# Cross-attention of a Perceiver block: value products in seven blocks of 9 and 10 tiles a head instead of eleven of 6, weighed 12 tiles later, and each head turned by transposes

## The chip, the cores and the metric

One core of one Trainium2 chip runs the whole program. The metric is device time in microseconds (us) of one launch, median of three runs; the profile is one further execution of the same program. The engines are TensorE (PE, with its weight loads as PEld), VectorE (DVE), ScalarE (ACT), GpSimd (POOL) and SyncE (SP, which only issues DMAs here).

## The reference, cut to what matters

Two Perceiver layers work on 512 tokens of width 512 with a context of 8192 tokens. Each layer is a cross-attention, a sequence mixer (a selective scan in the first, a delta rule in the second) and a mixture of experts. Only the two cross-attentions are touched:

```
q = layernorm(x) W_Q + b_Q ; k = ctx W_K + b_K ; v = ctx W_V + b_V      # 16 heads of 32
p = exp(q k^T / sqrt(32) - rowmax) ; head = (p v) / sum(p)               # 512 x 8192 per head
x = x + concat(heads) W_O + b_O
```

## The kernel before

Everything is in float32 accuracy. Queries and keys are split into a high and a low part and stacked, so that a score product has 96 or 97 rows of contraction. The engines run programs of their own, in the order in which the code issues them, and meet by semaphores; the order is written out by hand.

A head has KT = 64 tiles of 128 keys. For each tile, in the steady part of an attention:

- **first score** (`first_on_pe`, L775): queries by 512 keys, of the *next* head, 12 tiles ahead of where it must be finished; it goes into one of four PSUM banks. DVE takes its row maxima (L780), which is what frees the bank: PE's first score k waits for DVE's reading k-4.
- **second score** (`second_on_pe`, L797): 128 keys by 512 queries of this head, with the row maximum already subtracted by a 97th row of contraction (`qs`, filled by `send_row`). It goes into one of three banks; ACT takes the exponential into `pt` (L920), a ring of slots of 128x512. Second score n waits for exponential n-3.
- **weighing** (`weigh`): products of `pt` with the values, three tiles side by side on 32 columns of TensorE each (L810), and on the last 32 columns a product of ones with sums of `pt` (L814), which gives the sum of the exponentials. Three value products and one product of ones make a round; one round is two passes. All accumulate in one bank (`OUT_BANK`). To need one product of ones per round and not three, POOL first adds up the tiles of a block (`add_up`, L932 and L935) into `exp_sums`, which has two buffers.
- **end of a head**: ACT copies `OUT_BANK` to `partial` (`take_partial`, L902). PE multiplies it by a constant `fold` matrix (`finish_head`, L820), which adds the three column groups and turns the head at once: four products of 128x33 in two passes. DVE takes the reciprocal of the sum (L943), multiplies (L946) and adds the value bias (L950). PE may weigh block 0 of the next head only after L946 (`finished`).

Before, a block is 6 tiles (two rounds; two adds of 1024 elements on POOL), 11 blocks a head, the last of 4 tiles (one add). A block is weighed two blocks later (LAG = 2): PE does the 6 tiles of block b, first and second score in turn, and then weighs block b-2. The ring has 18 slots. `upto` tells up to which first score PE and DVE have come after each block.

In the last head there are no first scores left. There DVE does the adds of the odd blocks (`on_vector`), and PE does the first output products between the tiles (`output_early`, L858) after turning the rows of finished heads (`turn_heads`, L854, four 128x128 transposes; ACT copies them in `copy_turned`, L898). In head 0 ACT also writes four rows of ones into the keys of the other buffer (`ones_on_act`, L724), at tiles 12, 24, 36 and 48.

Of the kernel before, what the change touches and what calls it, by code (L numbers as in the profile page):

```python
# [9 lines left out]
ALU = mybir.AluOpType  # L10
# [497 lines left out]
class CrossAttention:  # L508
# [17 lines left out]
    RING = (LAG + 1) * BLOCK  # L526
    EARLY = UNITS + AHEAD
    ONES = (2, 4, 6, 8)
# [3 lines left out]
    EARLY_PRODUCTS = [(), (), (), (), (0,), (1,), (2,), (3,), (4,), (5, 6), (7, 8)]  # L532
    LATE_FIRST, LATE_NEXT, LATE_SCORES, NEXT_KEYS = 2, 2, 68, (8, 10)

    def __init__(self, c, A, S, x, l, late=None):
        self.c, self.A, self.S, self.x, self.l, self.late = c, A, S, x, l, late
        self.slots, self.upto = self.first_slots()
        self.begun, self.keys_stored = 0, []

    def adds(self, b):  # L540

        return -(-len(self.BLOCKS[b]) // self.ROUNDS) - 1

# [4 lines left out]
    def sums_to(self, h, b):  # L548

        mine = self.on_vector(h, b)  # L550
        n = sum(self.adds(j) for i in range(h + 1) for j in range(len(self.BLOCKS)) if (i, j) <= (h, b) and self.on_vector(i, j) == mine)
        return (self.sum_dve if mine else self.sum_pool).at(n)

    def slot(self, h, b):
        return (h * len(self.BLOCKS) + b) % (self.LAG + 1) * self.BLOCK

# [62 lines left out]
    def run(self):  # L619
        c, l = self.c, self.l  # L620
        with ExitStack() as st:
# [6 lines left out]
            self.bv = c.sb(st, f"bv{l}", [P, D])  # L628
# [8 lines left out]
            self.folded, self.inverse, self.finished, self.biased = c.signals(st, "head_folded total_inverse head_finished head_biased")  # L637
# [88 lines left out]
    def loads(self, sp):  # L726
# [8 lines left out]
        sp.dma_start(self.bv[:], self.A["bv"][self.l].partition_broadcast(P)).then_inc(*self.wo_in.up())  # L735
# [17 lines left out]

    def first_slots(self):


        units = [(h, i) for h in range(HEADS) for i in range(self.UNITS)]
        last = len(self.BLOCKS) - 1
        upto = {(h, b): min(len(units), self.UNITS + h * KT + tiles[-1] + 1 + self.AHEAD)
                - (self.BLOCK * (last - b) // last if h == 0 else 0)  # L760
                for h in range(HEADS) for b, tiles in enumerate(self.BLOCKS)}
        return units, upto
# [24 lines left out]
    def on_pe(self, pe):  # L787
# [11 lines left out]
        def weigh(h, b):  # L799
            tiles, slot, sums = self.BLOCKS[b], self.slot(h, b), (h * NB + b) % 2  # L800
            if b == 0:
                pe.wait_ge(*self.v_in[h % 2].at(h // 2 + 1))
            if b == 0 and h:
                pe.wait_ge(*self.finished.at(h))
            pe.wait_ge(*self.exp.at(h * KT + tiles[-1] + 1))
            if self.adds(b):
                pe.wait_ge(*self.sums_to(h, b))
            for r in range(self.ROUNDS):
                for g, i in enumerate(range(3 * r, min(3 * r + 3, len(tiles)))):
                    last = pe.matmul(bank[self.OUT_BANK][g * DH:(g + 1) * DH, :], vs[h % 2][:, tiles[i], :], pt[:, slot + i, :],  # L810
                                     start=b == 0 and r == 0, stop=tiles[i] + 3 >= KT)
                if r < len(tiles):
                    item = self.sums[:, sums, r, :] if self.adds(b) else pt[:, slot + r, :]
                    last = pe.matmul(bank[self.OUT_BANK][3 * DH:4 * DH, :], c.ones[:, 0:DH], item, start=b == 0 and r == 0, stop=b == NB - 1 and r == min(self.ROUNDS, len(tiles)) - 1)  # L814
            last.then_inc(*self.weighed.up())

        def finish_head(h):
            pe.wait_ge(*self.taken.at(h + 1))
            for t in range(TT):
                last = pe.matmul(bank[self.OUT_BANK][:, t * (DH + 1):(t + 1) * (DH + 1)], self.partial[:, t * P:(t + 1) * P], c.fold[:], start=True, stop=True)  # L820
            last.then_inc(*self.folded.up())

        def head(h):
            begun = self.upto[h - 1, NB - 1] if h else self.EARLY
# [6 lines left out]
            for b, tiles in enumerate(self.BLOCKS):  # L831
                todo = list(range(begun, self.upto[h, b]))
                begun = self.upto[h, b]
                for i, t in enumerate(tiles):
                    if todo:
                        self.first_on_pe(pe, todo.pop(0))
                    second_on_pe(h, t)
                    if i == 3 and h + 1 == HEADS:
                        output_early(b)
                    if i == 3 and b == self.LAG and h:  # L840
                        finish_head(h - 1)
                for k in todo:
                    self.first_on_pe(pe, k)
                if b >= self.LAG:
                    weigh(h, b - self.LAG)
                elif h:
                    weigh(h - 1, NB - self.LAG + b)

        def turn_heads(k):

            pe.wait_ge(*self.biased.at((k + 1) * HEADS // KD))
# [8 lines left out]
        def output_early(b):  # L860

            if b == 0:
                pe.wait_ge(*self.first_read.at(HEADS * self.UNITS))
            if b < self.EARLY_OUT:
                turn_heads(b)
            for i in self.EARLY_PRODUCTS[b]:
# [15 lines left out]
        for b in range(NB - self.LAG, NB):  # L882
            weigh(HEADS - 1, b)
# [8 lines left out]
    def on_act(self, act):  # L892
        NB = len(self.BLOCKS)

        def copy_turned(k):
            b = k if k < self.EARLY_OUT else self.SECOND_BANK + 1
            act.wait_ge(*self.at_turned.at(k + 1))
            act.copy(self.at[:, k, :], self.c.bank[b]).then_inc(*self.at_copied.up())  # L898
# [10 lines left out]
        for h in range(HEADS):  # L909
            for b, tiles in enumerate(self.BLOCKS):  # L910
                if b == self.LAG and h:
                    take_partial(h - 1)
                if h + 1 == HEADS and 2 <= b < 2 + self.EARLY_OUT:
                    copy_turned(b - 2)
                if h == 0 and b in self.ONES:
                    self.ones_on_act(act, 1, self.ONES.index(b))
                for i, t in enumerate(tiles):
                    n = h * KT + t
                    act.wait_ge(*self.second.at(n + 1))
                    act.activation(self.pt[:, self.slot(h, b) + i, :], self.c.bank[self.SECOND_BANK + n % self.SECOND_ROOM], ACT.Exp).then_inc(*self.exp.up())  # L920
# [3 lines left out]
    def add_up(self, engine, h, b, n, signal):  # L924

        tiles, g, slot, R = self.BLOCKS[b], h * len(self.BLOCKS) + b, self.slot(h, b), self.ROUNDS
        engine.wait_ge(*self.exp.at(h * KT + tiles[min((n + 2) * R, len(tiles)) - 1] + 1))
        to = self.sums[:, g % 2]
        if n == 0:
            if g > 1:  # L930
                engine.wait_ge(*self.weighed.at(g - 1))
            engine.tensor_tensor(to, self.pt[:, slot:slot + R, :], self.pt[:, slot + R:slot + 2 * R, :], ALU.add).then_inc(*signal.up())  # L932
        else:
            engine.wait_ge(*signal.at(signal.total - signal.base))
            engine.tensor_tensor(to, to, self.pt[:, slot + (n + 1) * R:slot + (n + 2) * R, :], ALU.add).then_inc(*signal.up())  # L935

    def on_dve(self, dve):
        bank = self.c.bank

        def finish_head(h):  # L940
            folded = bank[self.OUT_BANK][:, 0:TT * (DH + 1)].rearrange("p (t d) -> p t d", t=TT)
# [1410 lines left out]
```

## Time and profile before

| what | value |
|---|---|
| median of 3 runs | 3646.66 us (3643.27 to 3648.98) |
| the profiled execution, its own time | 3645.09 us |
| its span, first to last instruction | 3643.3 us (1.8 us lie around it) |
| mean granted TensorE clock | 0.984 |
| PE / DVE / ACT / POOL busy, share of the span | 97% / 69% / 54% / 49% |
| first attention, from its first second score to its last weighing | 700 to 1561 us |
| second attention | 1995 to 2855 us |

Busy shares over the whole span mix stages. The two attentions are some 1720 us of the 3643 us; the stages before, between and after them are the same in both kernels. A time such as 1101.51 is the start of an instruction in us from the start of the span; the second column of the order of time is how long it, or the run of equal instructions, took. A matmul's row is longer than its share of the engine, since matmuls overlap: what one costs is the distance between the starts of two.

### The profile page before, as it was taken

The numbers are of one execution on the slowest core, as the hardware profiler recorded it, in microseconds if no ns is written. First come the engines' busy times: TensorE is split into PE (matmuls) and PEld (weight loads), VectorE is DVE, ScalarE is ACT, GpSimd is POOL, SyncE is SP. The second block draws the span as 40 slices with busy tenths as digits, with TensorE's granted clock in tenths as the row PEclk, the third lists the DMA queues.
The fourth block names the chain that finished last, engine by engine and source line by source line (L and its number), as shares of the span: only waits on it lengthen the run. The fifth ranks groups of instructions, "written<-read, shape, count | busy, mean of one in ns | idle before, by whom it ended". The sixth has DMA issues, their size and how long they took to land. (4 is left out here: it accounts for less than half of the span.)

```text
span 3643.3 us, 47301 instructions
## 1 busy us (share of the span) xinstructions
PE 3527.5 (97%) x17916; PEld 2334.9 (64%) x17916; DVE 2497.3 (69%) x3465; ACT 1967.2 (54%) x3024; POOL 1773.3 (49%) x744
## 2 busy tenths in 40 slices
PE   8999999999999999988999999999999897999999
PEld 6788787755555555446876555555554476788887
DVE  3222344478777777457996777777775565899998
ACT  2122322366666666634972666666666322777786
POOL 2222222399999999700000999999998320100001
PEclk9999999999999999998998999999999998999999
DMA  7777776633333333046977433333330101999998
GB/s 272 253 243 235 234 239 208 190 79 91 93 90 77 88 93 77 15 174 223 359 302 238 122 92 84 80 93 93 80 91 24 53 1 53 361 377 374 374 375 302
DMA packets 249729, 628.50 MB, mean 173 GB/s; under 512 B 43633, under 2 KB 137873, under 8 KB 194977
## 3 DMA queue, kind: packets, MB, share of 16 engines
q1 hardware_dynamic: 210720, 552.08, 46.8%
q10 hardware_dynamic: 36864, 67.13, 5.0%
q0 software_dynamic: 1920, 6.29, 0.5%
q8 instruction: 143, 2.34, 0.3%
q14 instruction: 82, 0.66, 0.1%
HBM read 488.46 MB, written 136.87 MB: 172 GB/s over the span
## 5 line engine op out<-in xcount | busy, mean ns | idle before, releaser
L780 DVE TENSOR_REDUCE maxima<-psum 128x1 f32<-128x512 f32 x2048 | 1263.4, 680 | 359.3 <-PE psum L775 359.1
L920 ACT ACTIVATE pt<-psum 128x512 f32<-128x512 f32 x2048 | 1047.7, 612 | 590.6 <-PE psum L797 587.9
L932 POOL TENSOR_TENSOR exp_sums<-pt 128x1024 f32<-128x1024 f32 x342 | 819.3, 2396 | 259.2 <-ACT pt L920 136.9
L775 PE MATMUL psum<-ks,first_q 96*128 96x512 f32 x2048 | 852.4, 416 | 0.8
L797 PE MATMUL psum<-qs,ks 97*128 97x512 f32 x2048 | 817.7, 406 | 12.2 <-ACT pt L920 9.1
L935 POOL TENSOR_TENSOR exp_sums<-exp_sums,pt 128x1024 f32<-128x1024 f32 x310 | 735.7, 2373 | 44.5
L810 PE MATMUL psum<-pt,vs 128*32 128x512 f32 x4096 | 673.9, 598 | 2.1 <-POOL exp_sums L932 1.9
L814 PE MATMUL psum<-exp_sums,constants 128*32 128x512 f32 x1408 | 669.8, 598 | 0.0
L775 PEld LDWEIGHTS psum<-ks,first_q 96*128 96x128 f32 x2048 | 390.0, 190 | 354.2 <-DVE maxima L780 236.2
L1631 DVE TENSOR_TENSOR moe_cut<-moe_raw,moe_cut 128x2048 fp32r<-128x2048 f32 x244 | 556.8, 2289 | 55.9 <-ACT moe_cut L1627 49.5
L1627 ACT CAST moe_cut<-moe_raw 128x2048 fp32r<-128x2048 f32 x244 | 469.0, 1923 | 56.2 <-PE psum L97 47.3
L797 PEld LDWEIGHTS psum<-qs,ks 97*128 97x128 f32 x2048 | 390.7, 192 | 128.4 <-ACT pt L920 48.8
L372 POOL TENSOR_TENSOR cparts<-cx,cparts 128x2048 fp32r<-128x2048 f32 x32 | 147.7, 4615 | 522.3 <-ACT cparts L285 522.3
L810 PEld LDWEIGHTS psum<-pt,vs 128*32 128x32 f32 x4096 | 139.4, 109 | 342.3 <-issue 231.2
L1539 POOL DMA_INDIRECT ln_m_rows<-y_slots,row_of x8 | 14.0, 1747 | 666.4 <-DMA y_slots<-moe_yrow 664.6
L354 DVE SCALAR_TENSOR_TENSOR kparts<-psum,bk,kparts 128x512 fp32r<-128x512 f32 x128 | 96.0, 750 | 276.1 <-ACT kparts L311 276.1
L95 PE MATMUL psum<-moe_cut,moe_xg 128*128 128x512 f32 x608 | 241.6, 397 | 3.8 <-DVE moe_xg L1699 3.8
L97 PE MATMUL psum<-moe_cut,moe_xg 128*128 128x512 f32 x608 | 237.4, 390 | 0.0
L96 PE MATMUL psum<-moe_cut,moe_xg 128*128 128x512 f32 x608 | 236.6, 389 | 0.0
L95 PE MATMUL psum<-cparts,wk_high 128*128 128x512 f32 x512 | 205.7, 402 | 19.9 <-POOL cparts L372 16.9
L311 ACT ACTIVATE kparts<-psum,bk 128x512 fp32r<-128x512 f32 x128 | 88.0, 688 | 245.3 <-PE psum L97 221.9
L285 ACT CAST cparts<-cx 128x2048 fp32r<-128x2048 f32 x32 | 61.0, 1908 | 265.0 <-PE psum L97 178.4
(334 smaller groups left out, 4526.5 us busy)
## 6 DMA issues: line engine op xcount, KB each, us to landing
moe_raw<-in_moe_w SPq DMA_DIRECT2D x244, 1024.0 KB, 7.9
ks<-k_parts SPq DMA_DIRECT2D x384, 256.0 KB, 4.6
k_parts<-kparts ACTq DMA_DIRECT2D x256, 256.0 KB, 4.4
cx<-in_ctx SPq DMA_DIRECT2D x32, 1024.0 KB, 6.1
vs<-v_heads SPq DMA_DIRECT2D x32, 1024.0 KB, 5.3
v_heads<-vrow SPq DMA_DIRECT2D x25, 1024.0 KB, 5.1
late_context<-cparts SPq DMA_DIRECT2D x28, 512.0 KB, 11.6
late_parts<-late_context SPq DMA_DIRECT2D x28, 512.0 KB, 4.7
```

The source lines that it names most:

```text
L95: pe.matmul(out, lhs[0], rhs[0], start=start, stop=False)
L97: return pe.matmul(out, lhs[1], rhs[0], start=False, stop=stop)
L775: pe.matmul(self.c.bank[self.FIRST_BANK + k % self.FIRST_ROOM], self.first_q[s][:, t * P:(t + 1) * P], self.ks[s][part][0:3 * DH, at:at + ...
L780: dve.tensor_reduce(self.maxima[:, h % 2, i % TT, i // TT:i // TT + 1], self.c.bank[self.FIRST_BANK + k % self.FIRST_ROOM], X, ALU.max).th ...
L797: pe.matmul(bank[self.SECOND_BANK + n % self.SECOND_ROOM], ks[h % 2][part][:, at:at + P], qs[h % 2][:], start=True, stop=True).then_inc(*s ...
L810: last = pe.matmul(bank[self.OUT_BANK][g * DH:(g + 1) * DH, :], vs[h % 2][:, tiles[i], :], pt[:, slot + i, :], start=b == 0 and r == 0, st ...
L814: last = pe.matmul(bank[self.OUT_BANK][3 * DH:4 * DH, :], c.ones[:, 0:DH], item, start=b == 0 and r == 0, stop=b == NB - 1 and r == min(se ...
L920: act.activation(self.pt[:, self.slot(h, b) + i, :], self.c.bank[self.SECOND_BANK + n % self.SECOND_ROOM], ACT.Exp).then_inc(*self.exp.up())
L932: engine.tensor_tensor(to, self.pt[:, slot:slot + R, :], self.pt[:, slot + R:slot + 2 * R, :], ALU.add).then_inc(*signal.up())
L935: engine.tensor_tensor(to, to, self.pt[:, slot + (n + 1) * R:slot + (n + 2) * R, :], ALU.add).then_inc(*signal.up())
L1627: act.copy(self.cut[:, g % self.CUT, 0], self.raw[:, g % self.RAW]).then_inc(*self.high.up())
L1631: dve.tensor_tensor(self.cut[:, g % self.CUT, 1], self.raw[:, g % self.RAW], self.cut[:, g % self.CUT, 0].bitcast(F32), ALU.subtract).then ...
```

## The change

A block has nine tiles (three rounds) and the seventh and last has ten (four rounds, the last of one tile). POOL adds three tiles at once: two adds of 1536 elements a block, 14 a head. The product of ones of the tenth tile's round takes `pt` itself. A block is no longer weighed at a block's end but after the second score of the tile 12 behind its last tile, which is after tiles 20, 29, 38, 47 and 56 of the head and 1 and 11 of the next. The ring has 24 slots and the heads lie 66 slots apart, so that three tiles that are added together never wrap around. First scores are given out tile by tile (`first_to`), not block by block. In the diff below, the first `finish_head` is PE's and the second DVE's, which is now issued after the first score of tile 17 (`TURN + 1`); the lines with `later` are of `add_up`, whose n is 0 and 1.

The end of a head is done without `fold`: PE turns `partial` by four 128x128 transposes (after tile 16), DVE multiplies all three groups by the reciprocal into `scaled` and adds the groups by a reduction. Weighing the next head's block 0 waits for the multiplication (`divided`). The value bias is added later, as the bias of `copy_turned`. The row bias `x + b_O` in heads 0 to 3 stays. `SHARED` is empty, so no add is shared between POOL and DVE.

```diff
-    ROUNDS, LAG = 2, 2
+    ROUNDS, LAG = 3, 12
     BLOCK = 3 * ROUNDS
-    BLOCKS = [list(range(t, min(t + 3 * 2, KT))) for t in range(0, KT, 3 * 2)]
+    BLOCKS = [list(range(t, t + 3 * 3)) for t in range(0, KT - 10, 3 * 3)] + [list(range(KT - 10, KT))]
+    STRIDE, RING = 66, 24
+    TAKE, TURN = LAG, LAG + 4
+    SHARED, SHARE_AT = (), 3
-    RING = (LAG + 1) * BLOCK
-    ONES = (2, 4, 6, 8)
+    ONES = (12, 24, 36, 48)
+    COPY_AT = (10, 15, 20)
+    EARLY_AT = {3: (0, ()), 8: (1, ()), 13: (2, ()), 26: (None, (0,)), 32: (None, (1,)), 38: (None, (2,)), 43: (None, (3,)), 48: (None, (4,)), 53: (None, (5, 6)), 58: (None, (7, 8))}
...
+    def slot(self, h, t):
+        return (h * self.STRIDE + t) % self.RING
+    def due(self, h, t, late):
+        n = h * KT + t - late
+        return [(n // KT, b) for b, tiles in enumerate(self.BLOCKS) if n >= 0 and n % KT == tiles[-1]]
+    def first_to(self, h, t):
+        n = self.UNITS + h * KT + t + 1 + self.AHEAD - (6 * (KT - 1 - t) // (KT - 7) if h == 0 else 0)
+        return min(len(self.slots), max(self.EARLY, n))
...
         def finish_head(h):
             pe.wait_ge(*self.taken.at(h + 1))
             for t in range(TT):
-                last = pe.matmul(bank[self.OUT_BANK][:, t * (DH + 1):(t + 1) * (DH + 1)], self.partial[:, t * P:(t + 1) * P], c.fold[:], start=True, stop=True)
+                last = pe.transpose(bank[self.OUT_BANK][:, t * P:(t + 1) * P], self.partial[:, t * P:(t + 1) * P], c.ident[:])
...
+            for t in range(KT):
+                for k in range(begun, self.first_to(h, t)):
+                    self.first_on_pe(pe, k)
+                begun = self.first_to(h, t)
+                second_on_pe(h, t)
+                if h + 1 == HEADS and t in self.EARLY_AT:
+                    output_early(*self.EARLY_AT[t])
+                if t == self.TURN and h:
+                    finish_head(h - 1)
+                for block in self.due(h, t, self.LAG):
+                    weigh(*block)
...
-            act.copy(self.at[:, k, :], self.c.bank[b]).then_inc(*self.at_copied.up())
+            act.activation(self.at[:, k, :], self.c.bank[b], ACT.Identity, bias=self.bv[:, k:k + 1]).then_inc(*self.at_copied.up())
...
+        later = self.slot(h, tiles[3 * n + 3])
+        engine.wait_ge(*self.exp.at(h * KT + tiles[3 * n + 3] + hi))
+            engine.tensor_tensor(to, self.pt[:, first + lo:first + hi, :], self.pt[:, later + lo:later + hi, :], ALU.add).then_inc(*signal.up())
...
         def finish_head(h):
-            dve.tensor_tensor(rows, folded[:, :, 0:DH], self.total[:, :, None].to_broadcast([P, TT, DH]), ALU.mult).then_inc(*self.finished.up())
+            dve.tensor_tensor(self.scaled[:].rearrange("p t g d -> p t (g d)"), turned[:, :, 0:3 * DH], self.total[:, :, None].to_broadcast([P, TT, 3 * DH]), ALU.mult).then_inc(*self.divided.up())
+            dve.tensor_reduce(self.rows[:, :, h * DH:(h + 1) * DH], self.scaled[:].rearrange("p t g d -> p t d g"), X, ALU.add).then_inc(*self.finished.up())
-            dve.tensor_tensor(rows, rows, self.bv[:, None, h * DH:(h + 1) * DH].to_broadcast([P, TT, DH]), ALU.add).then_inc(*self.biased.up())
```

## Rows read from the trace of the kernel before

**Rows 1.** The page, busy time: engine, us, share of the span, instructions.

```profile
PE 3527.5 (97%) x17916; PEld 2334.9 (64%) x17916; DVE 2497.3 (69%) x3465; ACT 1967.2 (54%) x3024; POOL 1773.3 (49%) x744
```

**Rows 2.** Busy time by stretch: heads 1 to 14 of the first attention.

```profile
760.00:1490.00 730.00, 730.00 (x4205) 394.53 (x4205) 571.32 (x933) 454.47 (x888) 679.56 (x287) 1.00 0.33 84
```

**Rows 3.** Order of time on PE, one steady block.

```profile
1101.51 0.50 PE L775 MATMUL psum<-ks,first_q 96*128 96x512 f32 x1
1101.84 0.39 PE L797 MATMUL psum<-qs,ks 97*128 97x512 f32 x1
...
1104.18 0.40 PE L797 MATMUL psum<-qs,ks 97*128 97x512 f32 x1
...
1105.39 0.60 PE L810 MATMUL psum<-pt,vs 128*32 128x512 f32 x3
...
1105.82 0.60 PE L810 MATMUL psum<-pt,vs 128*32 128x512 f32 x3
...
1106.37 0.50 PE L775 MATMUL psum<-ks,first_q 96*128 96x512 f32 x1
```

**Rows 4.** Order of time, DVE and ACT beside that block.

```profile
1102.04 3.68 DVE L780 TENSOR_REDUCE maxima<-psum 128x1 f32<-128x512 f32 x6 [1.18 <-PE psum L775]
...
1102.27 3.05 ACT L920 ACTIVATE pt<-psum 128x512 f32<-128x512 f32 x6 [1.81 <-PE psum L797]
```

**Rows 5.** Order of time on DVE: a head's first block, an end of head, six heads on.

```profile
1130.23 3.68 DVE L780 TENSOR_REDUCE maxima<-psum 128x1 f32<-128x512 f32 x6 [1.43 <-PE psum L775]
...
1142.62 0.29 DVE L946 TENSOR_TENSOR head_rows<-psum,total 128x128 f32<-128x128 f32 x1
1142.94 1.79 DVE L950 TENSOR_TENSOR head_rows<-head_rows,bv 128x128 f32<-128x128 f32 x1
...
1450.60 3.68 DVE L780 TENSOR_REDUCE maxima<-psum 128x1 f32<-128x512 f32 x6 [1.43 <-PE psum L775]
```

**Rows 6.** Order of time on PE: fold in head 8, transposes in head 15.

```profile
1141.39 0.97 PE L820 MATMUL psum<-constants,partial 128*128 128x33 f32 x8
1142.20 0.48 PE L775 MATMUL psum<-ks,first_q 96*128 96x512 f32 x1
...
1503.96 0.60 PE L854 MATMUL psum<-constants,head_rows 128*128 128x128 f32 x4
1504.31 0.79 PE L797 MATMUL psum<-qs,ks 97*128 97x512 f32 x2
```

**Rows 7.** Costliest groups, whole trace: busy and mean ns, idle before.

```profile
L372 POOL TENSOR_TENSOR cparts<-cx,cparts 128x2048 fp32r<-128x2048 f32 x32 | 147.7, 4615 | 522.3 <-ACT cparts L285 522.3
L785 DVE TENSOR_REDUCE neg_max<-maxima 128x4 fp32r<-128x64 f32 x32 | 7.1, 220 | 1.1
L974 DVE TENSOR_TENSOR x_rows<-psum,x_rows 128x512 f32<-128x512 f32 x8 | 5.4, 678 | 8.3 <-PE psum L858 8.3
```

**Rows 8.** Order of time on POOL, first adds of two blocks without a wait.

```profile
1480.38 2.40 POOL L932 TENSOR_TENSOR exp_sums<-pt 128x1024 f32<-128x1024 f32 x1
...
1485.25 2.42 POOL L932 TENSOR_TENSOR exp_sums<-pt 128x1024 f32<-128x1024 f32 x1
```

**Rows 9.** Order of time in head 0 of the second attention, tile 12.

```profile
2003.36 1.89 ACT L724 CAST ks<-constants 1x2048 fp32r<-1x2048 f32 x1
...
2005.93 0.50 PE L797 MATMUL psum<-qs,ks 97*128 97x512 f32 x1 [1.35 <-ACT pt L920]
```

**Rows 10.** Order of time, last head of the first attention: ACT's step, then its end.

```profile
1495.06 3.05 ACT L920 ACTIVATE pt<-psum 128x512 f32<-128x512 f32 x6 [1.40 <-PE psum L797]
1499.50 2.07 ACT L920 ACTIVATE pt<-psum 128x512 f32<-128x512 f32 x4 [1.40 <-PE psum L797]
...
1551.95 2.07 ACT L920 ACTIVATE pt<-psum 128x512 f32<-128x512 f32 x4 [1.43 <-PE psum L797]
1556.85 2.36 POOL L932 TENSOR_TENSOR exp_sums<-pt 128x1024 f32<-128x1024 f32 x1 [5.95 <-PE psum L814]
1561.32 0.59 ACT L902 COPY partial<-psum 128x512 f32<-128x512 f32 x1 [7.30 <-PE psum L814]
```

More of the change, by code:

```diff
@@ L799, in weigh @@
         def weigh(h, b):
[L800 removed]
+            tiles, sums = self.BLOCKS[b], (h * NB + b) % 2
             if b == 0:
@@ L803, in weigh @@
             if b == 0 and h:
-                pe.wait_ge(*self.finished.at(h))
+                pe.wait_ge(*self.divided.at(h))
             pe.wait_ge(*self.exp.at(h * KT + tiles[-1] + 1))
[L806 to L814, printed above, removed]
+            if not self.on_vector(h, b):
+                pe.wait_ge(*self.sum_pool.at(self.sums_by_pool(h, b)))
+            if self.on_vector(h, b) or self.shared(h, b):
+                pe.wait_ge(*self.sum_dve.at(self.sums_by_dve(h, b)))
+            rounds = [tiles[i:i + 3] for i in range(0, len(tiles), 3)]
+            for r, three in enumerate(rounds):
+                for g, t in enumerate(three):
+                    pe.matmul(bank[self.OUT_BANK][g * DH:(g + 1) * DH, :], vs[h % 2][:, t, :], pt[:, self.slot(h, t), :], start=b == 0 and r == 0, stop=t + 3 >= KT)
+                item = self.sums[:, sums, r, :] if r < self.ROUNDS else pt[:, self.slot(h, three[0]), :]
+                last = pe.matmul(bank[self.OUT_BANK][3 * DH:4 * DH, :], c.ones[:, 0:DH], item, start=b == 0 and r == 0, stop=b == NB - 1 and r == len(rounds) - 1)
             last.then_inc(*self.weighed.up())
@@ L881, in on_pe @@
             head(h)
-        for b in range(NB - self.LAG, NB):
-            weigh(HEADS - 1, b)
+        for t in range(KT, KT + self.LAG):
+            for block in self.due(HEADS - 1, t, self.LAG):
+                weigh(*block)
         finish_head(HEADS - 1)
@@ L909, in on_act, with add_up @@
         for h in range(HEADS):
-            for b, tiles in enumerate(self.BLOCKS):
-                if b == self.LAG and h:
+            for t in range(KT):
+                n = h * KT + t
+                if t == self.TAKE and h:
                     take_partial(h - 1)
[L913 to L920, printed above, removed]
+                if h + 1 == HEADS and t in self.COPY_AT:
+                    copy_turned(self.COPY_AT.index(t))
+                if h == 0 and t in self.ONES:
+                    self.ones_on_act(act, 1, self.ONES.index(t))
+                act.wait_ge(*self.second.at(n + 1))
+                act.activation(self.pt[:, self.slot(h, t), :], self.c.bank[self.SECOND_BANK + n % self.SECOND_ROOM], ACT.Exp).then_inc(*self.exp.up())
         take_partial(HEADS - 1)
         copy_turned(KD - 1)
[L924 to L928, printed above, removed]
+    def add_up(self, engine, h, b, n, signal, parts=range(3)):
+        g, tiles, lo, hi = h * len(self.BLOCKS) + b, self.BLOCKS[b], parts[0], parts[-1] + 1
+        later = self.slot(h, tiles[3 * n + 3])
+        to = self.sums[:, g % 2, lo:hi]
+        engine.wait_ge(*self.exp.at(h * KT + tiles[3 * n + 3] + hi))
         if n == 0:
@@ L931, in add_up @@
                 engine.wait_ge(*self.weighed.at(g - 1))
[L932 to L935 removed]
+            first = self.slot(h, tiles[0])
+            engine.tensor_tensor(to, self.pt[:, first + lo:first + hi, :], self.pt[:, later + lo:later + hi, :], ALU.add).then_inc(*signal.up())
+        else:
+            engine.tensor_tensor(to, to, self.pt[:, later + lo:later + hi, :], ALU.add).then_inc(*signal.up())
     def on_dve(self, dve):
@@ L2239, in perceiver @@
         const = c.sb(ctx, "constants", [P, CONST_COLS])
-        c.ident, c.ones, c.iota, c.upto, c.lower, c.level0, c.fold, c.spare = (
-            const[:, CONST_AT[n][0]:CONST_AT[n][1]] for n in ("ident", "ones", "iota", "upto", "lower", "level0", "fold", "spare"))
+        c.ident, c.ones, c.iota, c.upto, c.lower, c.level0, c.spare = (
+            const[:, CONST_AT[n][0]:CONST_AT[n][1]] for n in ("ident", "ones", "iota", "upto", "lower", "level0", "spare"))
         c.level_t = [const[:, CONST_AT["level_t"][0] + k * P:CONST_AT["level_t"][0] + (k + 1) * P] for k in range(LEVELS)]
```

113 lines of the change are left out of this document (47 added, 66 removed).

## The prediction

> **What bounds the kernel now.** I read the page's busy times first: PE is busy for 97% of the span, and no other engine comes near [rows 1]. That share says nothing of a stage, so I went to the busy time by stretch. In heads 1 to 14 PE is busy for all of the 730 us at the full clock (1.00, the 2.4 GHz level), POOL for 679.56 (93%), DVE for 78%, ACT for 62%, the DMA engines for 33% [rows 2]. So PE sets the attention's pace, with POOL close behind it. The chain of waits adds nothing there, since PE waits for nobody. What a block costs PE is read from the order of time [rows 3]: the block repeats after 1106.37 - 1101.51 = 4.86 us. Eleven starts of scores in turn lie (1104.18 - 1101.84)/10 = 0.234 us apart, and one pass of weighing takes 1105.82 - 1105.39 = 0.43. Twelve scores (2.81) and four passes (1.72) make 4.53, so 0.33 us of each block is neither: it is the change from scores to weighing and back (the first score after weighing stands 0.33 ahead of the second and not 0.234, the rest lies at the two edges). Six heads take 1450.60 - 1130.23 = 320.37 us, 53.4 a head [rows 5]. The sum for one: 128 scores 30.0, 44 passes 18.9, 11 changes 3.6, end of head 0.8, together 53.3. The steady part is understood.
>
> **The change, part by part.**
>
> *Blocks.* 64 tiles in threes are 22 rounds before and after, so the number of products stays. The changes between scores and weighing go from 11 to 7 a head. Up to tile 51 of head 14, where first scores end, a layer weighs 14x11+7 = 161 times before and 14x7+4 = 102 after: 59 x 0.33 = 19.5 us, for two layers **-39.1 us** (0.331 unrounded). All of it lies on PE's path.
>
> *Longer runs between two weighings.* Runs of 6 become runs of 9, one of 10. PE steps by 0.469 a tile, DVE by (3.68-0.68)/5 = 0.60 and ACT by (3.05-0.61)/5 = 0.488 [rows 4], so both fall behind in a run and recover in the weighing. DVE starts 0.53 after the first score; first score k (from 0) wants to start at 0.10+0.469k and needs reading k-4, which ends at 0.53+0.60(k-4)+0.68. They meet at k = 9.8, at 9.4 with 0.06 us for the semaphore; the longest run has k = 9. For ACT, with three banks, they meet beyond k = 20. Cost taken: 0; if the slack of DVE fails, below.
>
> *POOL.* Without a wait two adds of 1024 take 1485.25 - 1480.38 = 4.87 us [rows 8]. An add of 2048 elements took 4.615 us elsewhere [rows 7], against 2.40, so 512 more elements cost 1.11. A pair of 1536 then takes 4.87+2.2 = 7.1, at most 1.5x4.87 = 7.3. PE needs 18x0.234+6x0.43+0.33 = 7.12 for nine tiles and 8.45 for the block of ten. Seven pairs are 49.7 (51.1) us a head against PE's 51.8 (53.4 less 4x0.33 and 0.46, plus 0.2, as below): POOL stays behind PE. A pair can begin with the sixth exponential of its block and is wanted about 9.1 us later (two runs and the weighing between them, less what leads up to it), so a drift of 0.18 a block is absorbed. Cost 0. The Trainium skill (Perfetto Trace Analysis, GPSIMD Engine Instruction) says that spans of GpSimd are unreliable and that start-to-start spacing is to be used; by the spans a pair before would be 4.8, by spacing it is 4.87, which is what I take, and neither makes POOL the bound.
>
> *End of a head on PE.* The fold keeps the next score off for 1142.20 - 1141.39 = 0.81 us, four transposes of the same size for 1504.31 - 1503.96 = 0.35 [rows 6]. 28 heads end in the steady part: 28x0.46 = **-12.9 us**; at 0.60 for the transposes it would be -6.
>
> *The wait on DVE.* PE may weigh block 0 only after the multiplication. It now has 384 elements: between 128 (0.29, [rows 5]) and 512 (0.678, [rows 7]) that is 0.55. In the run of tiles 12 to 20, DVE has read tile 17's scores 0.53+3.68 = 4.21 after the run's start, the reciprocal takes 0.2, the multiplication 0.55, a semaphore about 0.06: 5.03. PE comes to the weighing at 0.33+8x0.469+0.35+0.09+0.33 = 4.86. So a new stall of 0.2 us a head, 28x0.2 = **+5.6 us** (0 to 0.5 a head: 0 to 14). Behind that wait stand the rest of PE's queue; ACT and DVE have idle time there. The reduction that follows reads 384 elements of SBUF; one of 64 took 0.22 on the mean of 32 beside a busy POOL [rows 7], one of 512 some 0.68 (the short runs of [rows 4] end so), so some 0.55, where the bias add that goes had 1.79 [rows 5]. DVE has 1.5 us a run to spare, so neither counts.
>
> *The row bias add of heads 0 to 3* has two inputs in SBUF, as the bias add that goes away. That one, small as it is, took 1.79 because it waited for POOL's running add [rows 5]. The row bias add will now meet adds of 3.5 us. In its place POOL's first add of block 1 ends some 0.4 us after DVE gets there, and DVE is back before PE needs it: 0; if it waits for the second add too, 2.5 us eight times, 20 us. The Trainium skill (SBUF — State Buffer, "Who interferes with whom") says that a DVE instruction with two SBUF inputs contends with a GpSimd one that reads SBUF, and that a reduction does not on this chip; the trace agrees on both. If that were wrong for the reduction, see the third rival.
>
> *Ones in head 0.* Before, the copies at tiles 24, 36 and 48 stand behind a weighing, where ACT is idle. Now tile 24 is fourth in a run. A copy of 1.89 in the middle of a run held PE for 1.35 [rows 9] (tile 12, in both kernels). Tile 36 is seventh, and its late exponentials are wanted only after the weighing. Two layers: **+3 us**. Head 0 also has its first weighing after 21 tiles, not 18; three more tiles at DVE's step instead of PE's: 3x0.13x2 = **+1 us**.
>
> *The last head.* Here ACT is the slower one: a block of six steps by 1499.50 - 1495.06 = 4.44 us, with 1.40 idle during weighing [rows 10]. Nine tiles with three rounds: 4.44+3x0.488+0.86 = 6.76, against 6.66; over 76 tiles +0.8. The three copies of turned heads now stand in the middle of runs, each 0.5 on ACT's path, before mostly in its idle time: +1.2. At the end, before, the last exponential is done at 1554.02, and the copy of the head starts at 1561.32, 7.3 later. After, POOL's first add can start four tiles before the last exponential is done (-1.95), two adds take 7.15, and from its end to the copy it was 1561.32 - 1559.21 = 2.11 for four passes, so 3.83 for eight: 9.0, +1.7. The transposes and the longer DVE end give back 0.5. Together 3.2 a layer, **+6.5 us** (2 to 12).
>
> The bias on the copy of turned heads costs nothing visible: it is one ACT instruction for another. The smaller load of the bias is off the path.
>
> **Sum.** -39.1-12.9+5.6+3+1+6.5 = -35.9 us. On the profiled execution's own 3645.09 that gives 3609; that execution lies 1.6 below the median of 3646.66, so the forecast is 3611.
>
> **The rivals.**
> 1. *DVE's four banks don't carry the longer runs.* For: DVE's step is 28% longer than PE's, and the slack at k = 9 is only 0.05 to 0.1 us by the sum above. Against: at k = 5 the slack before is 0.6, and no wait shows. If nothing beyond six tiles were covered, 22 tiles a head would cost 0.13 each, 2.9 us a head, 30 heads 88 us, and the kernel would be slower (3699). It decides from 1.6 us a head on. The likelier form is a part of it, 0.1 to 0.2 a run, or a longer wait for the multiplication: 3623 to 3640.
> 2. *POOL becomes the pace*, the other side. If three tiles at once cost more per element (a pair over 7.4 us), PE waits in `weigh` for POOL; over 7.63 (53.4/7) the head is longer than before. At 7.8: 54.6 a head, +1.2x30, 3683. For: POOL is 93% busy. Against: the add of 2048 at 2.25 ns an element, below 2.34 for 1024.
> 3. *The reduction waits for POOL as the old bias add did.* In the gap between POOL's adds it costs nothing; waiting out the second add it is some 2.3 us a head, 28 heads 64 us: 3675.
> 4. *More than the sum*: no stall at the multiplication, last head at its lower end: -46, 3600 or just below.
>
> **How the numbers follow.** Forecast (3600 to 3622) 0.71; a partial stall of the first rival 0.13, its full form 0.03; POOL 0.04; the reduction 0.03; better 0.06. The likeliest is 3611. From 3600 I reach up to 3632, which takes in the upper bounds of the unknown costs (8 more at the wait, 7 at the transposes, 6 in the last head) and the nearer half of the partial stall. A change within 0.2% (7.3 us) is about what this measurement can't tell from none: faster than 3639.4 for 0.88, between for 0.04, slower for 0.08.
>
> **What the profile after would show.** A steady head of 51.8 us; nine tiles every 7.12 us on PE; no idle time of PE before first and second scores, and 0.2 us of it before block 0 is weighed; POOL adds of 3.5 us with small waits for ACT, not PE waiting for POOL; 102 weighings before the last stretch. The prediction is wrong if a switch does not cost 0.33 in the longer block (then nine tiles take over 7.2), if PE shows waits for DVE in runs, or if POOL's pair is over 7.4.

## The result and the profile after

The changed kernel takes 3618.73 us (median of 4 runs, 3611.42 to 3621.58), the kernel before beside it 3644.97: ratio 0.9925 (95% interval 0.9912 to 0.9937), which is 26 us less by the medians and 27 by the ratio. Forecast were 3611 and 36 less, in a range of 3600 to 3632. Two more series of the same kernel gave 0.9925 and 0.9924. The profiled execution took 3621.58 us, its span is 3619.6, 23.7 below the span before.

The page after, busy times, and the stretch that answers to [rows 2]:

```profile
PE 3495.2 (97%) x17788; PEld 2344.2 (65%) x17788; DVE 2462.6 (68%) x3457; ACT 1956.6 (54%) x3024; POOL 1751.4 (48%) x528
```

```profile
760.00:1442.00 682.00, 681.16 (x3989) 381.99 (x3991) 533.85 (x898) 431.03 (x855) 641.49 (x185) 1.00 0.35 88
```

PE is busy throughout as before, at the full clock; POOL has 94%. The page's 528 and 744 count all of POOL's instructions; the adds of exponentials among them are now 436 (2 x 218, shown below) and were 652. Next, the order of time on PE, one steady run of nine tiles with its weighing, beside [rows 3]:

```profile
1101.49 0.50 PE L785 MATMUL psum<-ks,first_q 96*128 96x512 f32 x1
1101.82 0.40 PE L807 MATMUL psum<-qs,ks 97*128 97x512 f32 x1
...
1105.58 0.39 PE L807 MATMUL psum<-qs,ks 97*128 97x512 f32 x1
1105.90 0.63 PE L823 MATMUL psum<-pt,vs 128*32 128x512 f32 x3
...
1108.61 0.50 PE L785 MATMUL psum<-ks,first_q 96*128 96x512 f32 x1
```

1108.61 - 1101.49 = 7.12 us for nine tiles, where the sum said 7.12: eighteen starts of scores 0.234 apart (4.21), six passes of 0.43 (2.58) and 0.33 for the change. The eight steps between second scores are (1105.58 - 1101.82)/8 = 0.470 each, so PE does not wait within the run. The next run is longer, 1115.91 - 1108.61 = 7.30. DVE in it, against [rows 4], shows why: the reduction for the row maximum (L795) falls among its readings, so the ninth first score waits for its bank. It starts 0.30 after the second score ahead of it and the second score after it another 0.34, where each was 0.23; together these are the 0.18, within the rounding:

```profile
1109.16 2.48 DVE L790 TENSOR_REDUCE maxima<-psum 128x1 f32<-128x512 f32 x4 [1.66 <-PE psum L785]
1111.67 0.22 DVE L795 TENSOR_REDUCE neg_max<-maxima 128x4 fp32r<-128x64 f32 x1
1111.81 3.07 DVE L790 TENSOR_REDUCE maxima<-psum 128x1 f32<-128x512 f32 x5
```

```profile
1112.24 0.40 PE L807 MATMUL psum<-qs,ks 97*128 97x512 f32 x1
1112.54 0.50 PE L785 MATMUL psum<-ks,first_q 96*128 96x512 f32 x1
1112.88 0.39 PE L807 MATMUL psum<-qs,ks 97*128 97x512 f32 x1
...
1115.91 0.49 PE L785 MATMUL psum<-ks,first_q 96*128 96x512 f32 x1
```

The end of a head on DVE, beside [rows 5], with reciprocal, multiplication of 384 elements and reduction (0.17, 0.56, 0.60, forecast 0.2, 0.55, 0.55):

```profile
1132.06 3.68 DVE L790 TENSOR_REDUCE maxima<-psum 128x1 f32<-128x512 f32 x6 [2.44 <-PE psum L785]
1135.66 0.17 DVE L951 RECIPROCAL total<-psum 128x4 f32<-128x4 f32 x1
1135.86 0.56 DVE L953 TENSOR_TENSOR scaled<-psum,total 128x384 f32<-128x384 f32 x1
1136.45 0.60 DVE L955 TENSOR_REDUCE head_rows<-scaled 128x128 f32<-128x384 f32 x1
```

And on PE, beside [rows 6]: the four transposes keep the next score off for 1134.32 - 1133.96 = 0.36 us, and the weighing of block 0 starts 0.46 after the last second score and not 0.33, so it waits 0.13 for the multiplication:

```profile
1133.96 0.60 PE L831 MATMUL psum<-constants,partial 128*128 128x128 f32 x4
1134.32 0.51 PE L785 MATMUL psum<-ks,first_q 96*128 96x512 f32 x1
...
1136.06 0.40 PE L807 MATMUL psum<-qs,ks 97*128 97x512 f32 x1
1136.52 0.63 PE L823 MATMUL psum<-pt,vs 128*32 128x512 f32 x3
```

POOL's groups on the page show 3.49 us for an add of 1536 elements (forecast 3.50), and that POOL waits for exponentials. PE waits for POOL 6.9 us in all, at the ends of the two attentions:

```profile
L941 POOL TENSOR_TENSOR exp_sums<-pt 128x1536 f32<-128x1536 f32 x218 | 760.8, 3490 | 275.2 <-ACT pt L927 270.1
L943 POOL TENSOR_TENSOR exp_sums<-exp_sums,pt 128x1536 f32<-128x1536 f32 x218 | 761.8, 3494 | 17.2
L823 PE MATMUL psum<-pt,vs 128*32 128x512 f32 x4096 | 652.7, 599 | 8.7 <-POOL exp_sums L943 6.9
```

The end of the first attention, in order of time, against [rows 10]:

```profile
1534.65 2.56 ACT L927 ACTIVATE pt<-psum 128x512 f32<-128x512 f32 x5 [1.10 <-PE psum L807]
...
1538.87 3.42 POOL L943 TENSOR_TENSOR exp_sums<-exp_sums,pt 128x1536 f32<-128x1536 f32 x1
...
1542.43 0.63 PE L823 MATMUL psum<-pt,vs 128*32 128x512 f32 x3 [3.44 <-POOL exp_sums L943]
...
1544.78 1.14 PE L823 MATMUL psum<-pt,vs 128*32 128x512 f32 x3
1545.63 1.14 PE L823 MATMUL psum<-pt,vs 128*32 128x512 f32 x3
...
1547.81 0.59 ACT L910 COPY partial<-psum 128x512 f32<-128x512 f32 x1 [10.60 <-PE psum L825]
```

From the last exponential (1537.21) to the copy of the head it is 10.6 us; before it was 7.3, forecast were 9.0. PE waits 3.44 us for POOL's two adds. After that wait its passes lie 0.43 us apart at first and then 0.85 (1545.63 - 1544.78): the granted clock has gone to its 1.2 GHz level. Busy time by stretch shows 0.68 for these 5.4 us:

```profile
1542.40:1547.80 5.40, 5.34 (x28) 1.58 (x28) 0.00 (x0) 0.00 (x0) 0.00 (x0) 0.68 0.01 3
```

Before the change PE waited there too, but only 0.97 us, and the passes after it lay 0.43 apart:

```profile
1559.35 0.63 PE L810 MATMUL psum<-pt,vs 128*32 128x512 f32 x3 [0.97 <-POOL exp_sums L932]
...
1559.78 0.63 PE L810 MATMUL psum<-pt,vs 128*32 128x512 f32 x3
```

ACT's copies of the heads to `partial` cut every trace into the same stretches. The table has them for all kernels, in us (the experiments are described below). Head 0 counts from the first second score; "steady head" is the mean of the 13 from the copy of head 0 to that of head 13, second attention.

| kernel | steady head | head 0, 2nd att. | head 0, 1st att. | heads 14, 15, 2nd att. |
|---|---|---|---|---|
| before | 53.48 | 63.20 | 64.60 | 51.57, 49.88 |
| after | 52.01 | 64.85 | 69.98 | 50.97, 53.20 |
| after_again | 52.02 | 64.84 | 67.00 | 51.01, 53.17 |
| after_third | 52.02 | 64.27 | 70.41 | 51.03, 53.19 |
| blocks_only | 52.34 | 64.97 | 68.81 | 52.97, 53.11 |
| transposes_only | 53.36 | 63.22 | 67.87 | 51.44, 49.90 |
| split_rounds | 54.51 | 66.58 | 68.61 | 51.77, 52.78 |
| turn_14 | 53.64 | 64.96 | 67.01 | 53.33, 53.19 |
| ones_behind | 52.04 | 62.29 | 65.32 | 52.73, 53.19 |
| last_on_dve | 52.02 | 64.90 | 67.04 | 50.98, 48.02 |
| ahead_16 | 51.85 | 65.41 | 69.29 | 52.42, 53.18 |
| three_edits | 51.85 | 62.50 | 66.87 | 52.34, 48.04 |

The steady heads gain 1.47 x 13 = 19.1 us in each attention. Head 0 gives back 1.65 in the second attention, head 15 3.3, head 14 gains 0.6: -14.7 in all. The first attention gains 11.0, since its head 0 is 5.4 longer. Outside the attentions the profiled execution is 2.0 longer.

One difference in the last column isn't the code's alone. In some attentions head 14 takes 52.3 to 53.3 us instead of 51.0 to 51.8, and then its mean clock is 0.97 and not 1.00. That is so in 9 of the 20 attentions of kernels with the new blocks (in one of the changed kernel's own six), and in none of the four of `before` and transposes_only. No wait of PE over 0.4 us stands in such a head (ones_behind, 1439 to 1496 us), so what brings the clock down there stays open.

### The profile page after: what moved, and what is told of

The parts are those of the page before. It is cut to its first block and busy times, and to the rows that moved or that the text cites. A ratio compares the mean times of both kernels' runs of the same rounds, so it can differ in the third digit from the quotient of the medians.

```text
span 3619.6 us, 46469 instructions
## 1 busy us (share of the span) xinstructions
PE 3495.2 (97%) x17788; PEld 2344.2 (65%) x17788; DVE 2462.6 (68%) x3457; ACT 1956.6 (54%) x3024; POOL 1751.4 (48%) x528
## 5 line engine op out<-in xcount | busy, mean ns | idle before, releaser
L927 ACT ACTIVATE pt<-psum 128x512 f32<-128x512 f32 x2048 | 1036.0, 625 | 520.6 <-PE psum L807 518.0
L941 POOL TENSOR_TENSOR exp_sums<-pt 128x1536 f32<-128x1536 f32 x218 | 760.8, 3490 | 275.2 <-ACT pt L927 270.1
L943 POOL TENSOR_TENSOR exp_sums<-exp_sums,pt 128x1536 f32<-128x1536 f32 x218 | 761.8, 3494 | 17.2
L823 PE MATMUL psum<-pt,vs 128*32 128x512 f32 x4096 | 652.7, 599 | 8.7 <-POOL exp_sums L943 6.9
L825 PE MATMUL psum<-exp_sums,constants 128*32 128x512 f32 x1344 | 622.6, 599 | 0.0
L823 PEld LDWEIGHTS psum<-pt,vs 128*32 128x32 f32 x4096 | 156.4, 110 | 377.1 <-issue 313.8
```

Source lines behind the costliest of these rows:

```text
L927: act.activation(self.pt[:, self.slot(h, t), :], self.c.bank[self.SECOND_BANK + n % self.SECOND_ROOM], ACT.Exp).then_inc(*self.exp.up())
L941: engine.tensor_tensor(to, self.pt[:, first + lo:first + hi, :], self.pt[:, later + lo:later + hi, :], ALU.add).then_inc(*signal.up())
L943: engine.tensor_tensor(to, to, self.pt[:, later + lo:later + hi, :], ALU.add).then_inc(*signal.up())
```

## The experiments

**after_again, after_third: the changed kernel once more.** No edit.

> The changed kernel once more, for the clock. In the profile after, the granted clock stood at the 1.2 GHz level for 20.5 us from the start of the first attention, before the change for 10.2 us, and again for 3.4 us where the end of each attention waits for POOL. Theory: the steady head takes 52.0 us again, and the 3.4 us at the end of each attention comes back, since the wait before it does; the length at the start is chance, so it may be 10 or 20 us, and the first head of the first attention then takes 66 or 70 us. Rival: the longer low stretch belongs to the change and is 20 us again in every profile of it, head 70 us, and it explains 4 us of the shortfall by itself. Time 3612 to 3621 either way.

> The changed kernel beside it, on the same chip: 0.9925 of the kernel before, steady head 52.0. Its low-clock stretch at the start of the first attention is 10 or 20 us by chance (one more profile for that count).

Measured: 3615.75 us (ratio 0.9925, 0.9912 to 0.9939) and 3619.09 (0.9924, 0.9911 to 0.9938). The steady head is the same to 0.01 us. Head 0 of the first attention took 67.00 and 70.41. Busy time by stretch of the first 40 us of that attention, the clock in the third column from the right; in this order after, after_again, after_third:

```profile
697.60:737.60 40.00, 37.64 (x154) 21.66 (x155) 24.59 (x39) 28.37 (x45) 27.25 (x8) 0.75 0.66 175
```

```profile
697.60:737.60 40.00, 36.69 (x166) 21.45 (x166) 27.09 (x44) 30.79 (x50) 29.66 (x9) 0.87 0.66 175
```

```profile
698.00:738.00 40.00, 37.52 (x152) 21.16 (x153) 24.05 (x38) 27.77 (x44) 26.78 (x8) 0.74 0.67 174
```

The same kernel has 0.74, 0.75 or 0.87 there, and its head 0 is 3 us longer at the lower ones. transposes_only had 0.76, with blocks as before. So the longer low stretch doesn't need the change, and the change doesn't always bring it. How often either kernel has it can't be said from one profile each of before and the variants. The mean clock of whole runs says a little more: 25 runs of the kernel before have 0.982 to 0.985 (mean 0.984), the 14 of the changed kernel 0.980 to 0.983 (mean 0.982). By my estimate the two low stretches at the ends of the attentions, 3.4 us each at half the clock, make 0.001 of that; the other 0.001, some 4 us, is not accounted for. So chance alone at the start is not shown either. The low stretch behind the wait for POOL was there at both ends in all three profiles; it begins between at once and some 1.3 us after the end of the wait, and costs about four passes of 0.43.

**blocks_only: the end of a head as before.**

```diff
-                last = pe.transpose(bank[self.OUT_BANK][:, t * P:(t + 1) * P], self.partial[:, t * P:(t + 1) * P], c.ident[:])
+                last = pe.matmul(bank[self.OUT_BANK][:, t * (DH + 1):(t + 1) * (DH + 1)], self.partial[:, t * P:(t + 1) * P], c.fold[:], start=True, stop=True)
...
+            dve.tensor_tensor(rows, rows, self.bv[:, None, h * DH:(h + 1) * DH].to_broadcast([P, TT, DH]), ALU.add).then_inc(*self.finished.up())
```

> The changed kernel with the end of a head as before: fold products on PE, multiplication of 128 elements and bias add on DVE. Theory: PE loses 0.46 us a head at the fold and gets back the 0.15 us that it now waits for the longer multiplication: 52.3 us a head against 52.0, 28 heads +9 us, so about 3628. Rival: the longer multiplication, the reduction and the transposes together cost what the fold did (DVE is late by them for the rest of the run), so the head stays at 52.0 and the time within 3 us of the changed kernel. A third way: the bias add waits for a POOL add of 3.5 us now, not 2.4, and DVE holds PE up: over 52.6 a head, over 3637.

Measured: 3628.00 us (ratio 0.9959, 0.9945 to 0.9973), steady head 52.34. The theory holds: the new end of a head is worth 0.32 us of each, the new blocks the rest, 53.48 - 52.34 = 1.14 (from head 5 on 53.39 - 52.33 = 1.06). Four changes fewer (1.32) less the 0.17 of the long run are 1.15 by the sum, so no gain is left over for the later weighing, the larger ring and the first scores tile by tile, which came with the blocks. The bias add took 1.14 us on DVE in head 8 (in order of time from 1140.20), less than the 1.79 before. In both kernels it ended about 0.15 us after the end of the POOL add that was running when it started (1141.19 here, 1144.58 before), so what it takes depends on where in POOL's add it starts.

**transposes_only: the other half alone, on the kernel before.** The same lines the other way round.

> The kernel before with the end of a head by transposes, multiplication of 384 elements and reduction, blocks of 6 as before. Theory: PE saves 0.46 us, but the head is turned after the fourth tile of a run and block 0 is weighed after the sixth, so PE comes to it at 0.33+5*0.469+0.44+0.33 = 3.45 us after the run's start and DVE is through at 3.01+0.2+0.55+0.06 = 3.82: it waits 0.37. Head 53.3 against 53.4, time 3640 to 3645. Rival: the transposes carry a good part of the change's gain by themselves (0.46 a head and no wait), 53.0 a head, 3633.

Measured: 3637.98 us (ratio 0.9989, 0.9980 to 0.9998), steady head 53.36, and from head 5 on 53.27 to 53.33, against 53.35 to 53.43 before. The saved 0.46 us of fold is nearly all lost to the wait for the multiplication, as the sum of the theory had it (0.37): in the order of time on PE block 0 is weighed 1142.89 - 1142.21 = 0.68 us after the last second score and not 0.33. Most of the change is the blocks.

**split_rounds: the changes between scores and weighing put back, nothing else.** `SPLIT` is (1, 2, 3, 4).

```diff
-                for block in self.due(h, t, self.LAG):
-                    weigh(*block)
+                for r in range(3):
+                    for i, b in self.due(h, t, self.LAG + 3 * r):
+                        if b in self.SPLIT:
+                            weigh(i, b, r)
+                        elif r == 0:
+                            weigh(i, b)
```

> The changed kernel with blocks 1 to 4 of each head weighed in three pieces, one round each, after the tiles 12, 15 and 18 behind the block's last one, and not three rounds at a stretch. Nothing is added but changes between scores and weighing: 8 more a head. Theory (a change costs 0.33 us): +2.65 us a head, less 0.16 for the shorter runs where DVE no longer is late: 54.5 a head, 30 heads +75 us, about 3694. Rival (the blocks' gain comes from elsewhere, from fewer and longer adds on POOL, and the change between scores and weighing hides): 52.0 a head, 3619. In between, a change costs less when a single round stands between scores.

Measured: 3684.72 us (ratio 1.0119, 1.0103 to 1.0134), steady head 54.51, where the theory said 54.5. The order of time on PE has a piece of three tiles with one round in 1109.40 - 1106.80 = 2.60 us: six scores 1.40, two passes 0.86, and 0.34:

```profile
1106.80 0.50 PE L786 MATMUL psum<-ks,first_q 96*128 96x512 f32 x1
...
1109.40 0.50 PE L786 MATMUL psum<-ks,first_q 96*128 96x512 f32 x1
```

POOL's adds are the same here as in the changed kernel, so their number is not what the change gains from; the price of a change is what it is. The total is 69 us over the changed kernel (3615.75) and not 75, since only 26 steady heads have all eight: 26 x 2.49 are 65, and head 0 and head 14 add 1.7 and 0.8 in the second attention.

**turn_14: DVE's end of head earlier in the run.**

```diff
-    TAKE, TURN = LAG, LAG + 4
+    TAKE, TURN = LAG, LAG + 2
```

> The changed kernel with the head turned after tile 14 and not 16, DVE's end of head after tile 15's scores. Theory of the four banks: PE no longer waits 0.15 us for the multiplication, but DVE's 1.3 us now stand after the fourth reading of the run; its fifth ends at 3.0+1.3+0.68 = 5.0 us after the run's start, and the ninth first score, which wants to start at 4.3, waits for it: +0.75-0.15, so 52.6 us a head against 52.0. Rival: only the wait for the multiplication counts, since DVE has idle time in each run: 51.9 us a head.

Measured in one run: 3665.38 us. From head 5 on a head takes 52.67 to 52.84, near the 52.6 of the four banks. Heads 1 to 4, where DVE also does the row bias add, take 54.78 to 56.53, which neither theory had. In the order of time on DVE that add (L959) takes 2.12 us in head 1, in the changed kernel 1.01, and the same within 0.03 in the other seven; the first fence is turn_14, with the POOL add that was running, the second the changed kernel:

```profile
766.28 3.46 POOL L941 TENSOR_TENSOR exp_sums<-pt 128x1536 f32<-128x1536 f32 x1 [0.99 <-ACT pt L927]
768.17 2.12 DVE L959 TENSOR_TENSOR x_rows<-x_rows,bo 128x512 f32<-128x512 f32 x1
```

```profile
772.88 1.01 DVE L959 TENSOR_TENSOR x_rows<-x_rows,bo 128x512 f32<-128x512 f32 x1
```

It ends at 770.29, behind the end of POOL's add at 769.74, and PE waits 2.62 us for DVE. In the next head the wait is the same, but what follows it is not:

```profile
770.95 0.63 PE L785 MATMUL psum<-ks,first_q 96*128 96x512 f32 x1 [2.62 <-DVE maxima L790]
...
772.79 1.07 PE L823 MATMUL psum<-pt,vs 128*32 128x512 f32 x3
773.65 1.07 PE L823 MATMUL psum<-pt,vs 128*32 128x512 f32 x3
...
827.33 0.50 PE L785 MATMUL psum<-ks,first_q 96*128 96x512 f32 x1 [2.63 <-DVE maxima L790]
...
828.44 0.61 PE L823 MATMUL psum<-pt,vs 128*32 128x512 f32 x3
828.87 0.61 PE L823 MATMUL psum<-pt,vs 128*32 128x512 f32 x3
```

Passes are 0.86 us apart after the first wait and 0.43 after the second. Busy time by stretch for the two heads has the clock at 0.97 and at 1.00:

```profile
763.90:820.30 56.40, 53.77 (x307) 29.14 (x305) 42.48 (x69) 32.90 (x65) 49.12 (x15) 0.97 0.33 82
820.30:875.20 54.90, 52.27 (x306) 29.02 (x306) 42.49 (x69) 32.95 (x66) 49.18 (x15) 1.00 0.33 85
```

PE's wait is 2.62 to 2.65 us in all eight such heads; five of them have 0.97 and take 56.3 to 56.5 us, three have 1.00 and take 54.8. So the add costs 2 us a head by itself, and another 1.6 where the clock falls. The prediction had priced a late row bias add at 2.5 us a head and taken it as 0: at tile 16 the phase is good, at tile 14 it isn't.

**ones_behind, last_on_dve, ahead_16: one loss each.** Each is a single run without a run of the changed kernel beside it, so the stretches of its trace are read and not its time. The edits in this order:

```diff
-    ONES = (12, 24, 36, 48)
+    ONES = (21, 30, 39, 48)
...
-        return h + 1 == HEADS and b % 2 == 1
+        return h + 1 == HEADS and b % 2 == 0
...
-    AHEAD = 12
+    AHEAD = 16
```

> The changed kernel with ACT's four copies of ones in head 0 at tiles 21, 30, 39 and 48, each first after a weighing, and not at 12, 24, 36 and 48. Theory: the copies at tiles 12 and 24 each hold PE for 1.35 to 1.5 us in the second attention's first head, which goes from 64.8 to 62.0 to 63.3 us (the lower if DVE then keeps up in the long first run), and all other heads stay. Rival: ACT and DVE are so far behind in the first run of 21 tiles that the copies hide behind DVE: 64.5 or more.

Measured: head 0 of the second attention 62.29 us against 64.84 (3618.35 us in one run). The two waits of PE in that head, which the changed kernel's order of time shows, are gone:

```profile
1994.65 0.50 PE L807 MATMUL psum<-qs,ks 97*128 97x512 f32 x1 [1.60 <-ACT pt L927]
...
2005.33 0.50 PE L807 MATMUL psum<-qs,ks 97*128 97x512 f32 x1 [1.36 <-ACT pt L927]
```

The first is of tile 12 and was there before the change [rows 9]; the second, of tile 24, is new. What was gained did not show in the one time taken: head 14 was 1.6 and 1.8 longer in the two attentions, for a low stretch of the clock there (0.97 on the mean of the head).

> The changed kernel with the last head's blocks 0, 2, 4 and 6 added up by DVE and 1, 3 and 5 by POOL, the other way round. Theory: the last weighing waits 3.4 us for POOL's two adds of 3.5 us, and the clock falls to its 1.2 GHz level in that wait, which doubles four passes (+1.7). With DVE's adds of 1.76 us the wait goes and with it the low stretch: last head 48.0 us against 53.2 in both attentions, -10 us in all. Rival: the clock falls there anyway, as PE's share of busy time is low in the whole last head: 49.7. Second rival: DVE's adds wait for POOL's, or another end is late next: 51 or more.

Measured: last head 48.02 us in both attentions, and 3607.62 us in one run. The wait for POOL and the low stretch behind it are both gone: in the order of time the last passes lie 0.43 us apart and the copy follows 0.67 us after the last pass starts:

```profile
1539.06 0.59 PE L823 MATMUL psum<-pt,vs 128*32 128x512 f32 x1
1539.49 0.59 PE L823 MATMUL psum<-pt,vs 128*32 128x512 f32 x1
```

So the clock fell for the wait, and not for PE's lower share of busy time in the whole last head. Three_edits, below, shows it again in both attentions.

> The changed kernel with first scores 16 tiles ahead and not 12, so that the reduction for the row maximum comes after the ninth reading of a run (tile 47), where DVE is idle next, and not after the fourth (tile 51). Theory: that run takes 7.12 us like the others and not 7.30: 51.85 us a head against 52.02. Rival: the 0.17 us are lost elsewhere in the head (at the longest run, or where POOL's adds begin), and the head stays at 52.0. Four first scores move from the first attention's last head to the stage before it, at no cost to the sum.

Measured: steady head 51.85 us, as said; the time of the one run, 3620.51, doesn't show it. Head 14 was 1.3 and 1.4 longer, again with the clock at 0.97 in it.

**three_edits: these three together.**

> The changed kernel with three of the edits together: ones at tiles 21, 30, 39 and 48, the last head's blocks 0, 2, 4 and 6 on DVE, first scores 16 tiles ahead. Theory: they sit in different stretches and add up. 13 heads of 51.86 and not 52.02 in each attention (-4), head 0 shorter by 1.7 and 2.6 (-4), last head 48.0 and not 53.2 (-10): 18 us below the changed kernel, ratio to the kernel before 0.9875, about 3597 beside a kernel before of 3642.6. Rival: what is gained at one place is lost again to the granted clock, whose low stretches differ from run to run: within 10 us of the changed kernel, 3606 or more.

Measured: 3602.49 us (ratio 0.9884, 0.9869 to 0.9899), 16.6 below the changed kernel's 3619.09 beside it, where 18 were expected (as a ratio 0.9875, as a time 3597). The single stretches came as said: steady head 51.85, head 0 62.50, last head 48.04. Head 14 has 52.36 and 52.34 and not 51.0, with the clock at 0.97; that takes back 2.7 us, which is the rival in part. This is the fastest version.

## Why the prediction came out as it did

- **What bounds the kernel**: PE, before and after. Right.
- **Blocks, 0.33 us for each change between scores and weighing**: right in mechanism and size. The run of nine took the 7.12 us of the sum, and eight changes put back cost 2.49 us a head, which is 8 x 0.33 less the 0.17 below. One miscount: the trace before has 160 weighings up to the last first score of a layer and not 161, so the term is -38.4 and not -39.1.
- **End of a head on PE**: 0.45 us forecast less, 0.36 against 0.81 measured. Right.
- **The wait for the multiplication**: 0.2 us forecast, 0.13 to 0.15 measured. Blocks_only gives the balance of this and the last point as 0.32 us a head, the forecast had 0.26.
- **Longer runs, cost 0**: this step was too low. I set DVE's readings against four banks and found 0.05 to 0.1 us of slack at the ninth score, but left out that in one run of each head the reduction for the row maximum stands among them. The term was taken as 0 and measured 0.17 us a head (ahead_16), some 5 us in all. The run of ten took 1131.52 - 1123.02 = 8.50, against 8.45. The first rival named this form of loss, with 0.1 to 0.2 us for every run; it is one run in seven. In that run PE does wait for DVE, which the prediction had named as a sign of being wrong; but 0.17 us a head is a tenth of the 1.6 from which it would have decided.
- **POOL**: 3.49 us an add, no wait of PE in the steady part. Right; the second rival fell. In split_rounds its adds are unchanged and the time is not.
- **The reduction beside POOL**: 0.60 us each time (591 to 608 ns over 32), so it doesn't wait; the third rival fell. The row bias add takes 1.0 and costs PE nothing at tile 16 (heads 1 to 4 take 51.9 to 52.1 us like the others). What I had not counted: heads 1 to 4 were 0.27 us longer than the others before (53.6 to 53.7 against 53.4) and no longer are, a gain of 2 us.
- **Head 0**: +2 us a layer forecast for the copy of ones (1.5) and the longer first run (0.5), less four changes (1.3): +0.7. Measured +1.65 in the second attention. The new wait at tile 24 is 1.36, near the 1.5 forecast; the rest, 1.65 + 1.3 - 1.36 = 1.6, stands against the 0.5 for the first run. Whether all of it is that run of 21 tiles wasn't taken apart.
- **The last head**: +3.2 us forecast, with the end at 9.0 us from the last exponential to the copy; measured +3.3 for head 15 with 10.6 at the end. The sum was right by luck: I had POOL's lateness, but not that the clock falls behind it and slows four passes (1.6 us), and I had counted 1.5 too much elsewhere in the head.
- **The sum**: -35.9 forecast. The spans of three profiles of the changed kernel lie 23.7, 28.0 and 25.9 below the one of before, the runs' ratio says 27. Of the 9 missing, the steady heads are 3 (20.5 forecast and 19.1 measured in each attention), and the second attention's head 0 and the last two heads of both some 2. The first attention's head 0 is 2.4 to 5.8 us longer than in before's one profile where 0.7 were forecast, so it is short by 1.7 to 5.1. The larger part of that is the clock at the start in two of the three profiles. Whether it belongs to the change is not settled: the changed kernel also has the low stretch short, and a kernel with the old blocks has it long, but over all runs the changed kernel's clock is lower than the waits at the ends explain. That 27 lies near 36 at all rests on the right price and count of the changes; the terms that were too low are the clock and the waits of DVE and of the first run.

## What to carry to other kernels

Where two kinds of products alternate on TensorE, look at the starts on either side of the seam and not at the busy share: eight pairs of seams a head at 0.33 us each, put back, cost 69 us, 2% of this kernel, with TensorE "busy" for all of it. Longer runs are paid by whoever reads the banks, so put every extra instruction of that reader (a row maximum, an end of a head) where a run ends, and work out for the k-th product which reading it needs. And when a helper's operations get longer, look at the last one before the end of the stage: nothing is behind it to cover it, and the wait can take the clock along.

## What the runs showed of the hardware

- The change from score products (96 or 97 rows by 128 columns) to products on 32 columns and back cost 0.34 us with one round between (split_rounds), 0.33 with two (before) and 0.33 with three (after).
- A wait of TensorE for POOL of 3.44 us (4.14 in split_rounds) at the end of an attention was followed by a stretch at the 1.2 GHz level, with passes 0.85 us apart and not 0.43, in all 16 ends of the eight profiles that have it. Without the wait the clock stayed up (four ends, last_on_dve and three_edits), and so it did after a wait of 0.97 (before and transposes_only, four ends). After waits of 2.62 to 2.65 us in mid-attention (turn_14) the clock fell in five heads of eight.
- The low stretch of the clock at the start of the first attention was shorter or longer in different executions of one kernel (0.74, 0.75 and 0.87 on the mean of the first 40 us), worth 3 us. In head 14 the clock was at 0.97 in some attentions without a wait of TensorE over 0.4 us.
- A DVE add of 128x512 with two inputs in SBUF took 0.68 us between two of POOL's adds (before, 769.81, POOL free from 769.74 to 770.57), 1.00 to 1.03 beside an add that was nearly through (after, eight times), and 2.12 to 2.14 beside one with 1.6 us to go (turn_14, eight times). A reduction of 384 elements in SBUF took 0.59 to 0.61 in all 32 cases.
- POOL's adds of two SBUF inputs took 2.40 us for 1024 elements, 3.49 for 1536 and 4.62 for 2048.
